# The segment sums of a graph layer's tail: from 8 wide matmul instructions a step to 16 narrow ones in two column halves, with 26 instead of 24 steps whose source rows TensorE selects

## The reference, cut to what matters

```python
def _L0_gnn_ref(x, edge_index, gamma, beta, W1, b1, W2, b2):
    mean = jnp.mean(x, axis=0)
    var = jnp.mean(jnp.square(x - mean), axis=0)
    xn = (x - mean) * jax.lax.rsqrt(var + BN_EPS) * gamma + beta
    xi, xj = xn[dst], xn[src]                       # 200000 edges, 6250 nodes, 64 channels
    h = jax.nn.relu(jnp.concatenate([xi, xj - xi], axis=-1) @ W1 + b1)   # 128 wide
    msg = h @ W2 + b2                               # 64 wide
    agg = jax.ops.segment_max(msg, dst, num_segments=N_NODES)
    agg = jnp.where(jnp.isfinite(agg), agg, 0.0)
    return jax.nn.relu(agg)
x = _layernorm(x + _L0_gnn_ref(...), axis=-1)
```

## Time and profile before

| | |
|---|---|
| median of 3 runs | 1803.86 us (1803.62 to 1804.23) |
| the profiled execution's own time | 1801.84 us |
| its span, first to last instruction | 1800.1 us |
| TensorE busy | 1721.3 us, 96% |
| GpSimd busy | 1317.6 us, 73% |
| VectorE busy | 1197.9 us, 67% |
| ScalarE busy | 939.6 us, 52% |
| mean granted TensorE clock | 0.977 |

### The profile page before, as it was taken

The page is one execution under the profiler, slowest core; times in us unless marked ns, Lnnn a source line. Parts: engine busy times, 40 slices in busy tenths (PEclk is TensorE's granted clock), DMA queues, the critical chain, the costliest instruction groups (busy, mean ns, idle before and its releaser), DMA issues.

```text
span 1800.1 us, 26957 instructions
## 1 busy us (share of the span) xinstructions
PE 1721.3 (96%) x9871; PEld 851.8 (47%) x9871; DVE 1197.9 (67%) x1951; ACT 939.6 (52%) x1111; POOL 1317.6 (73%) x1388
## 2 busy tenths in 40 slices
PE   4489999999999999999999999999999999999995
PEld 3244444444444444444444444444445445444442
DVE  5556676666766766667667667676676676666753
ACT  4545555545455545555555555555555555555553
POOL 7777777777777777777777777777777777777722
PEclk8589999999999999999999999999999999999998
DMA  7633343334334333343343333343333433343320
GB/s 180 176 94 93 67 98 88 75 82 96 79 82 97 72 96 79 86 96 67 85 94 96 83 82 93 73 95 70 97 89 65 104 83 85 79 99 81 70 55 5
DMA packets 131566, 156.85 MB, mean 87 GB/s; under 512 B 74988, under 2 KB 76969, under 8 KB 131400
## 3 DMA queue, kind: packets, MB, share of 16 engines
q1 hardware_dynamic: 85674, 109.73, 19.6%
q0 software_dynamic: 44464, 45.18, 17.0%
q10 hardware_dynamic: 1294, 0.20, 0.1%
HBM read 147.24 MB, written 9.39 MB: 87 GB/s over the span
## 4 chain that ended last, share of the span: by engine, by line
PE 94%; DVE 2%; SPq 1%; DMA 1%; ACT 1%; ACTq 1%; issue 0%; POOLq 0%; POOL 0%; DVEq 0%
PE ps_g L1074 29%; PE ps_g L1081 15%; PE ps_acc L1149 11%; PE ps_mr L1118 11%; PE ps_h L1140 10%; PE ps_mr L1124 5%; PE ps_h L1133 5%; PE ps_x L1110 4%; PE ps_h L1138 2%; DMA src_t<-in_src 1%; DMA a_dram<-oh 1%; DVE runmax L939 0%; PE ps_x L1037 0%; SPq L336 0%; SPq L351 0%
## 5 line engine op out<-in xcount | busy, mean ns | idle before, releaser
L473 POOL DMA_INDIRECT xs<-in_x,src_ix x1372 | 1304.8, 951 | 420.4 <-issue 417.3
L865 DVE TENSOR_SCALAR oh<-ps_k 128x1024 bf16<-128x1024 bf16 x1176 | 731.9, 679 | 0.8
L1074 PE MATMUL ps_g<-oh,xtab 128*128 128x512 bf16 x2352 | 541.1, 380 | 0.0
L635 ACT ACTIVATE rows<-ps_mr 128x512 f32<-128x512 f32 x196 | 116.8, 596 | 554.5 <-PE ps_mr L1124 545.1
L939 DVE TENSOR_TENSOR_SCAN runmax<-rb,runmax,ps_mr 128x512 f32<-128x512 bf16 x196 | 250.6, 1278 | 181.2 <-PE ps_mr L1118 180.3
L1074 PEld LDWEIGHTS ps_g<-oh,xtab 128*128 128x128 bf16 x2352 | 217.0, 98 | 301.9 <-issue 68.9
L640 ACT ACTIVATE hid<-ps_h,bias 128x1024 f32<-128x1024 f32 x196 | 218.2, 1113 | 175.0 <-PE ps_h L1140 139.1
L1081 PE MATMUL ps_g<-oh,xtab 128*64 128x512 bf16 x2352 | 289.7, 383 | 0.0
L922 DVE TENSOR_TENSOR best<-ps_acc,last_key 128x336 f32<-128x336 f32 x196 | 99.5, 508 | 282.0 <-PE ps_mr L1124 264.2
L1149 PEld LDWEIGHTS ps_acc<-rows,best 128*106 128x106 f32 x1568 | 183.0, 172 | 160.1 <-issue 155.8
L596 ACT ACTIVATE best<-best,ones 126x1024 bf16<-126x1024 bf16 x196 | 225.1, 1149 | 6.4
(11 more groups left out here) (162 smaller groups left out, 584.6 us busy)
## 6 DMA issues: line engine op xcount, KB each, us to landing
kb<-keys_dram SPq DMA_DIRECT2D x98, 504.0 KB
rb<-reset_dram SPq DMA_DIRECT2D x98, 256.0 KB
xs<-in_x,src_ix POOLq DMA_INDIRECT x1372
src_t<-in_src SPq DMA_DIRECT2D x48, 256.0 KB, 6.7
aw<-a_dram SPq DMA_DIRECT2D x196, 31.5 KB
a_dram<-oh SPq DMA_DIRECT2D x6, 672.0 KB, 3.9
xwin<-xp_dram SPq DMA_DIRECT2D x196, 10.5 KB
out<-y SPq DMA_DIRECT2D x182, 10.5 KB
```

Of the source, the lines that this page charges most:

```text
L473: pool.indirect_dma_start(xs[:, u, t, h, :], None, x[:, :], bass.IndirectOffsetOnAxis(ap=src_ix[:, b, q + t, h:h + 1], axis=0))\
L865: dve.tensor_scalar(oh[0:PN, n % NOH, :], node_keys_ps, n % TN + 0.5, None, ALU.is_equal).then_inc(oh_ready, 1)
L1074: last = pe.matmul(ps_g[:, h, :], xtab[0:PN, t, 0:2, :].rearrange("p w c -> p (w c)"), oh[0:PN, n % NOH, h * GE:(h + 1) * GE], start=t == ...
```

## The change

Three things:

- `sums_of` makes two calls a tile, one for each stream: 42 columns of weights against 65 columns of `rows` (the stream's 64 channels and a one), stream 0 into partitions 0 to 41 and stream 1 into partitions 64 to 105 of `ps_acc`. In the built program the calls carry the tile size 128 rows by 64 columns, at columns 0 and 64, as those of `messages` do. In a trace they are 16 matmul and 16 load instructions a step.
- A window now takes 65 columns, so a group's seven windows fit `ps_acc` (455 columns beside the 42 of the slot numbers), and `add_bias` runs once for each group (15 groups, the last two of them short) with one product and one addition over all 106 partitions. `rows` and `pick` are laid out to match; `ps_acc` is set to zero once at the start, in place of `best`.
- PICKED is 26, not 24: two steps fewer are gathered (16 gathers), and 98 more tiles are selected.

```diff
-    PICKED = 24
+    PICKED = 26
...
-    NR = 2 * C + 1
-    CUTS = (0, 3, 5, WB)
...
-        rows = sb("rows", [P, 2, TG, NR])
+        rows = sb("rows", [P, 2, TG * 2, C1])
...
-        pick = best[:, 5 * GE:7 * GE].rearrange("p (u n s) -> p u n s", u=2, s=64)
+        pick = best[:, 5 * GE:5 * GE + 2 * TG * 2 * SL].rearrange("p (u n s) -> p u n s", u=2, s=SL)
...
+        acc_v = ps_acc[0:ROWS, 0:WB * C1].rearrange("p (w c) -> p w c", c=C1)
...
-                    act.activation(rows[:, j % 2, :, 0:2 * C], ps_mr[:, :].rearrange("p (t c) -> p t c", t=TG),
+                    act.activation(rows[:, j % 2, :, 0:C], ps_mr[:, :].rearrange("p (t c) -> p t c", c=C),
...
+            chain(dve.memset(ps_acc[:, 0:GE - SL], 0.0))
...
-                def add_bias(c0, c1):
+                def add_bias(n, c0, c1):
                     wn = c1 - c0
-                    acc_v = ps_acc[:, 0:wn * NR].rearrange("p (w c) -> p w c", c=NR)
-                    dve.tensor_tensor(bias2[:, c0:c1, :], acc_v[0:ROWS, :, 2 * C:NR].to_broadcast([ROWS, wn, C]),
+                    dve.tensor_tensor(bias2[:, c0:c1, :], acc_v[:, c0:c1, C:C1].to_broadcast([ROWS, wn, C]),
...
-                    for p0, p1 in ((0, 64), (64, ROWS)):
-                        dve.tensor_tensor(sums[p0:p1, c0:c1, :], acc_v[p0:p1, :, p0:p0 + C], bias2[p0:p1, c0:c1, :], ALU.add).then_inc(added, 1)
+                    dve.tensor_tensor(sums[:, c0:c1, :], acc_v[:, c0:c1, 0:C], bias2[:, c0:c1, :], ALU.add).then_inc(added, 1)
...
-                    if k in sub_ends:
-                        add_bias(*sub_ends[k])
+                    if k in ends:
+                        add_bias(*ends[k])
...
                     for t in range(TG):
-                        last = pe.matmul(ps_acc[0:ROWS, q * NR:(q + 1) * NR], pick_cols[:, j % 2, t, 0:ROWS], rows[:, j % 2, t, :],
-                                         start=(i == 0 and t == 0), stop=(i == WI - 1 and t == TG - 1))
+                        for h in range(2):
+                            last = pe.matmul(ps_acc[h * 64:h * 64 + SL, p * C1:(p + 1) * C1], pick[:, j % 2, t * 2 + h, :],
+                                             rows[:, j % 2, t * 2 + h, :], start=(i == 0 and t == 0),
+                                             stop=(i == WI - 1 and t == TG - 1))
```

More of the change, by code:

```diff
@@ L78, in edge_conv_program @@
     gathered = [k for k in range(NI) if k not in picked]
-    sub_of, sub_ends = {}, {}
-    for w in range(NW):
-        a = max(c for c in CUTS if c <= w % WB)
-        sub_of[w] = w % WB - a
-        if w % WB + 1 in CUTS:
-            sub_ends[w * WI + WI + 2] = (a, w % WB + 1)
     ends = {w1 * WI + 2: (n, w0 % WB, w0 % WB + w1 - w0) for n, (w0, w1) in enumerate(GROUPS)}
@@ L196, in edge_conv_program @@
         onehot = best[0:SR, 3 * GE:5 * GE].bitcast(bf16).rearrange("p (u h e) -> p u h e", u=2, h=2)
-        pick = best[:, 5 * GE:7 * GE].rearrange("p (u n s) -> p u n s", u=2, s=64)
-        pick_cols = best[:, 5 * GE:7 * GE].rearrange("p (u t m) -> p u t m", u=2, t=TG)
+        pick = best[:, 5 * GE:5 * GE + 2 * TG * 2 * SL].rearrange("p (u n s) -> p u n s", u=2, s=SL)
         xp = best[:, 7 * GE:9 * GE].rearrange("p (h e) -> p h e", h=2)
@@ L725, in _ @@
                 dve.tensor_copy(src_ix[:, 0, q0:q1, :], first_ix[:, q0:q1, :]).then_inc(src_ix_ready, 1)
-            dve.memset(rows[:, :, :, 2 * C:NR], 1.0).then_inc(ones_ready, 1)
+            dve.memset(rows[:, :, :, C:C1], 1.0).then_inc(ones_ready, 1)
             dve.memset(eps_col[:, :], EPS).then_inc(ones_ready, 1)
@@ L865, in node_onehot @@
                     dve.tensor_scalar(oh[0:PN, n % NOH, :], node_keys_ps, n % TN + 0.5, None, ALU.is_equal).then_inc(oh_ready, 1)
-                def add_bias(c0, c1):
+                def add_bias(n, c0, c1):
                     wn = c1 - c0
-                    acc_v = ps_acc[:, 0:wn * NR].rearrange("p (w c) -> p w c", c=NR)
-                    dve.tensor_tensor(bias2[:, c0:c1, :], acc_v[0:ROWS, :, 2 * C:NR].to_broadcast([ROWS, wn, C]),
+                    dve.tensor_tensor(bias2[:, c0:c1, :], acc_v[:, c0:c1, C:C1].to_broadcast([ROWS, wn, C]),
                                       b2b[0:ROWS, :].rearrange("p (a c) -> p a c", a=1).to_broadcast([ROWS, wn, C]),
                                       ALU.mult).then_inc(added, 1)
-                    subs[0] += 1
-                    dve.wait_ge(added, subs[0] * 3 - 2)
-                    for p0, p1 in ((0, 64), (64, ROWS)):
-                        dve.tensor_tensor(sums[p0:p1, c0:c1, :], acc_v[p0:p1, :, p0:p0 + C], bias2[p0:p1, c0:c1, :], ALU.add).then_inc(added, 1)
+                    dve.wait_ge(added, n * 2 + 1)
+                    dve.tensor_tensor(sums[:, c0:c1, :], acc_v[:, c0:c1, 0:C], bias2[:, c0:c1, :], ALU.add).then_inc(added, 1)
                 def norm_sum(n, c0, c1):
                     wn = c1 - c0
-                    dve.wait_ge(added, subs[0] * 3)
+                    dve.wait_ge(added, n * 2 + 2)
                     dve.wait_ge(xwin_in, 32 * WB * min(n + 1, NW // WB))
@@ L905, in norm_scale @@
                                       ALU.mult).then_inc(y_ready, 1)
-                chain(dve.memset(best[:, 5 * GE:7 * GE], 0.0))
-                subs = [0]
                 n = 0
@@ L921, in _ @@
                             dve.wait_ge(last_ready, len(LAST_GROUPS))
-                        dve.tensor_tensor(pick[:, k % 2, :, 0:SL], slots_v,
+                        dve.tensor_tensor(pick[:, k % 2, :, :], slots_v,
                                           last_key[:, k - 2, :, :].rearrange("p t h -> p (t h)")
@@ L1145, in sums_of @@
                     w, i = divmod(j, WI)
-                    q = sub_of[w]
+                    p = w % WB
                     pe.wait_ge(pick_ready, j + 1)
                     for t in range(TG):
-                        last = pe.matmul(ps_acc[0:ROWS, q * NR:(q + 1) * NR], pick_cols[:, j % 2, t, 0:ROWS], rows[:, j % 2, t, :],
-                                         start=(i == 0 and t == 0), stop=(i == WI - 1 and t == TG - 1))
+                        for h in range(2):
+                            last = pe.matmul(ps_acc[h * 64:h * 64 + SL, p * C1:(p + 1) * C1], pick[:, j % 2, t * 2 + h, :],
+                                             rows[:, j % 2, t * 2 + h, :], start=(i == 0 and t == 0),
+                                             stop=(i == WI - 1 and t == TG - 1))
                     if j == NI - 1:
```

## The result

The changed kernel takes 1739.45 us (median of 4 runs, 1738.57 to 1741.0); the kernel before, beside it, 1803.74 (1803.44 to 1804.23). The ratio is 0.964, with a 95% interval of 0.963 to 0.966: 64 us faster. The forecast was 1739, its range 1733 to 1758. The profiled execution took 1739.88 us, with a span of 1738.1.

What follows compares the result with a forecast made beforehand. TensorE bounds the kernel: 1801.84 - 129.9 (sums) + 63.7 + 0.5 + 0.7 (picked steps) - 1.7 (start and end) = 1735.1 us. Meeting GpSimd's limit of 1736.5 makes 1737, and the 2.0 run offset 1739; range 1733 to 1758.

Steps and rivals of the forecast that it cites:

- The bound: TensorE, busy 96% of the span and 94% of the last chain: an instruction removed gains its full price.
- The sums: Sums in column halves side by side, fewer shape changes: 0.72 us a step, 0.51 where `wide` comes first, 129.9 in all.
- The two picked steps: 98 more tiles selected on TensorE at 0.65 us cost 63.7 us, plus 0.5 for picked steps and 0.7 for single-tile steps.
- GpSimd: Next limit: gathers each 1.25 us, the last at 1706.9; step 194's landing at 1699.6 puts the end at 1736.5 us.
- The tail: End of the program on TensorE: sums lose 0.5 and 0.9 us, one addition fewer saves 0.3, 1.7 us saved.
- The offset: Median of the runs 2.0 us over the profiled execution (1803.86 against 1801.84), added to 1737 to give 1739.
- The TensorE sum, 1735.1: TensorE's time without waits for gathers: 1801.84 - 129.9 + 63.7 + 0.5 + 0.7 - 1.7 us.
- The 1.9 for meeting gathers: Near the end TensorE's and GpSimd's limits lie 1.4 us apart and steps sometimes wait for both, raising 1735.1 to 1737.
- 1 (halves take turns, 1825): In the sums, small instructions don't overlap between column halves: 0.93 us a step replace 0.46, median 1825, slower; chance 0.12.
- 2 (open loads, 1801): Weight loads of the sums aren't hidden: slot 0.10, a step's sums 0.80 us, median 1801, no tellable change; chance 0.04.
- 3 (VectorE late at group ends, 1752): VectorE needs 10.0 us in group-end steps with 8 tiles, TensorE 9.1; carried into `turn`, 13 us: 1752; chance 0.04.
- 4 (clock, 1746): Waits for gathers thin TensorE's end work; its clock falls to 1.2 GHz steps sooner, 5 to 10 us: 1746; chance 0.08.

Runs made afterwards that it cites:

- the experiments at 24 and 25: The changed kernel with PICKED 24 or 25 in place of 26, new sums kept: 1762.67 us (ratio 0.977) and 1750.46 us (ratio 0.970).
- the kernel with three parts a group: The changed kernel with add_bias run three times a group again, after windows 3, 5 and 7, new layout kept: 1738.88 us, ratio 0.963.

## Why the prediction was right, and where it was not

**The bound.** TensorE was the bound, and stayed it: what was taken from its steps appeared in the time. The kernel with the old sums and 26 picked steps gives the sums' gain by itself: 127.8 us between the medians, 128.1 between the bodies, where 129.9 was predicted.

**The sums.** Slot 0.058 us, step 0.46, messages to `narrow` 1.36, with `wide` first 1.47: measured 0.46, 1.37 and 1.47. The step that could have failed in the prediction was taking the messages (512 columns) as the model for instructions of 65 columns. It held, and the experiment with the loops exchanged shows what it rested on, the issue order (0.26 us a step otherwise). The load row was the better guide than the sentence on loads of the Trainium skill's page. The 1.8 us by which the body's gain fell short lie in a few steps, where 0.72 or 0.51 were counted: the two with a single tile gave 0.39 us each, the two behind them 0.11, step 189 0.33 and step 17 nothing; step 2 isn't in the body.

**The two picked steps.** 64.9 us predicted, 63.1 measured between the medians and 64.1 between the bodies. Single-tile steps take 4.92 us, 4.95 predicted. A step behind such a one takes 9.31 us with 8 tiles, where others take 8.90, and step 189 waits 0.21 us for a one-hot tile: small losses that the sum hadn't. For steps 3 to 189 the terms make -65.0 and the traces show -64.0.

**GpSimd.** As the next limit it was right, and the experiments at 24 and 25 show how close. But the prediction had TensorE wait for gathers at steps 190 to 194, 2 to 6 us in all, and put 1.9 us on the sum for it. It waited for none. Step 194's last gather was issued at 1695.88, 1.0 us earlier than predicted, and had landed at 1698.4. TensorE's own sum, without gathers, puts that step's transposes at 1735.1 - 1.7 (around the span) - 35.2 (transposes to end: 36.9 less 1.7) = 1698.2; they came at 1699.6. So TensorE, 1.4 us late, was behind the gathers by a microsecond, and not the other way round. The prediction bounded the landing by the scatters' 3.4 us. That bound was wrong: the waits at 24 picked steps show 2.4 to 6.3 us, and 6.3 here would have had TensorE wait. That this one took 2.5 was luck.

**The tail.** This is the term that missed: -1.7 predicted, +1.1 in the profiled execution. The clock is 2.6 us of the 2.8 between them. From step 195's transposes to the last sums (1776.25 to 1783.69 before, 1712.76 to 1722.79 after) it is 7.44 us before and 10.03 after, with the same instructions, since the clock fell 25 us and not 16 us before the end. The rest is small: the last sums take 1.14 us to the product (1722.79 to 1723.93), where the prediction had 1.87 - 0.9 = 0.97. That this is a cost of the change, the runs don't show: the kernel with 64-column weights has the same end at 55.2 us, 0.9 less than before the change, with the clock at full speed until 15 us before the end. The prediction took the clock of one trace's end as fixed, and it differs between traces. Whether the new sums make an early fall more frequent (three of eight traces, none of two with the old sums) stays open.

**The offset.** The 2.0 us between profiled execution and median were added as if they belonged to the kernel. After the change the profiled execution lies 0.4 us above the median. That offset is the draw of one run among several that differ by up to 2.4 us.

So 1739 and 1739.45 agree better than the terms do. The TensorE sum, 1735.1, was 4.8 us short of the profiled 1739.88: +0.9 at the start, +1.0 in the body, +2.8 in the tail, 0.1 rounding. The start is no term of the change either: step 3's `turn` comes between 106.8 and 110.1 us in the traces of the experiments, at 108.7 with the old sums and 26 picked steps. The 1.9 for meeting gathers and the 2.0 of offset, which came in neither form, filled that hole. The mechanism and the size of its terms were right; that the last 4 us came out too was luck.

**The rivals.** 1 (halves take turns, 1825): out for this order; with the loops exchanged a good half of it comes true (47.6 of 86 us). 2 (open loads, 1801): out, by the 64-column loads. 3 (VectorE late at group ends, 1752): out, by the kernel with three parts a group, whose steps take the same. 4 (clock, 1746): its effect stands in one trace of the end, at 2.6 us, without the waits for gathers that were to cause it, and is absent from that with 64-column weights.

## What to carry to other kernels

Where small matmuls of two independent streams stand on the full array, look at whether each can have its own column half; issue the halves in turn, and beside instructions of the same shape, since the order and the neighbours were worth 48 and 45 of 128 us here. Compare kernels by the stretch between two fixed points in the middle of their traces: it repeats here to 0.1 us, where the end differs by 2 us with where the clock falls. When such a gain makes TensorE faster, compute when the engine that feeds it, busy share or not, is through: here two picked steps more cost 63 us of TensorE work where it was the bound, and at 26 of them the two engines met, 11 us below the kernel with one picked step fewer and 29 us below that with one more. Price an engine by its pace from start to start (a gather each 1.25 us), not by its busy share of 73%.

## What the runs showed of the hardware that was not expected

- TensorE starts instructions of the free column half ahead of earlier ones of the busy half, but only a few ahead: with eight of one half in a row, the other half began 0.23 us late, when three of the eight were still to start, and the 16 took 0.82 us up to `wide`, where the halves in turn take 0.56.
- A wait in the middle of the program can cost more than itself. After 3.56 us without work the next instructions ran at 1.2 GHz (1.97 us for 1.08).
- Loads of 64 columns took 138 ns by the records and of 42 columns 118 ns, in slots of 58 ns (0.46 us for 8): the loads' durations overlap each other too, and say nothing of the pace. The step grew by 0.01 us.
- From the issue of a step's last gather to the transposes that waited for it was 2.4 to 6.3 us over 35 waits of one trace; three of the six longest had no stores of the output near them, and the cause was not tested.
- At the end of the program, with all but the same instructions, the clock fell 25, 20 and 15 us before the end in three of the traces, and the end took 57.2, 55.9 and 55.2 us.
